# The last four row tiles of an adjacency product, cut in two groups of two instead of three and one

## The reference

```
keep   = u >= 0.1
x_drop = x * keep / 0.9
y      = x + adj @ x_drop
out    = (y - mean(y)) / sqrt(var(y) + 1e-5)      # over the 64 columns of each row
```

## Time and profile before

| | |
|---|---|
| median of 3 runs | 641.93 us (641.93 to 641.95) |
| profiled execution, its own time | 642.16 us |
| its span | 640.2 us |
| TensorE (PE) busy | 510.8 us, 80% |
| TensorE weight loads (PEld) | 263.7 us |
| VectorE busy | 60.8 us, 9% |
| ScalarE busy | 17.0 us, 3% |
| bytes moved by DMA | 274.80 MB, mean 429 GB/s |

### The profile page before, as it was taken

The page is one execution under the profiler, slowest core; times in us unless marked ns, Lnnn a source line. Parts: engine busy times, 40 slices in busy tenths (PEclk is TensorE's granted clock), DMA queues, the critical chain, the costliest instruction groups (busy, mean ns, idle before and its releaser), DMA issues.

```text
span 640.2 us, 7695 instructions
## 1 busy us (share of the span) xinstructions
PE 510.8 (80%) x3458; PEld 263.7 (41%) x3458; DVE 60.8 (9%) x268; ACT 17.0 (3%) x24; POOL 1.1 (0%) x8
## 2 busy tenths in 40 slices
PE   0088798798788787887788878878977977979997
PEld 0044444444443443443444434433433443445435
DVE  1200100100100100010100110010010020020202
ACT  0000000000000000000000000000000000000000
POOL 0000000000000000000000000000000000000000
PEclk9997988988988987989978978978977987979999
DMA  9999999999999999999999999999999999999998
GB/s 385 430 431 447 427 430 450 430 430 447 434 430 424 445 434 404 430 434 439 430 434 447 430 430 450 430 430 440 436 434 399 458 438 407 435 424 431 434 419 354
DMA packets 7348, 274.80 MB, mean 429 GB/s; under 512 B 944, under 2 KB 1072, under 8 KB 1456
## 3 DMA queue, kind: packets, MB, share of 16 engines
q1 hardware_dynamic: 7200, 274.70, 99.5%
q10 hardware_dynamic: 144, 0.03, 0.0%
HBM read 272.63 MB, written 2.10 MB: 429 GB/s over the span
## 4 chain that ended last, share of the span: by engine, by line
DMA 66%; PE 33%; issue 0%; SPq 0%; DVE 0%; ACT 0%; ACTq 0%; DVEq 0%
DMA adj_ring<-adj_blocks 66%; PE acc L234 31%; PE tail_acc L234 2%; PE back L241 0%; SPq L151 0%; PE final L273 0%; SPq L153 0%; DVE x_and_u L342 0%; SPq L172 0%; ACT std L224 0%; DVE acc_sb L280 0%; ACTq L202 0%; DVE stats L336 0%; DVE mean_var L338 0%; DVE rstd L340 0%
## 5 line engine op out<-in xcount | busy, mean ns | idle before, releaser
L234 PE MATMUL acc<-adj_ring,x_and_u 128*64 128x320 f32 x3072 | 463.9, 467 | 99.4 <-ACTq L202 99.4
L234 PEld LDWEIGHTS acc<-adj_ring,x_and_u 128*64 128x64 f32 x3072 | 232.1, 148 | 326.2 <-ACTq L202 107.3
L280 DVE COPY acc_sb<-acc 128x320 f32<-128x320 f32 x24 | 10.7, 486 | 477.0 <-PE acc L234 477.0
L234 PE MATMUL tail_acc<-adj_ring,x_and_u 128*64 128x384 f32 (+1 forms) x256 | 29.1, 382 | 0.9 <-DMA adj_ring<-adj_blocks 0.8
L241 PE MATMUL back<-twofold,acc_sb 128*128 128x64 f32 x126 | 16.8, 280 | 11.9 <-DVE acc_sb L280 11.9
L196 ACT ACT_TABLE_LOAD x10 | 12.8, 1283 | 502.5 <-DMA adj_ring<-adj_blocks 502.5
L241 PEld LDWEIGHTS back<-twofold,acc_sb 128*128 128x128 f32 x126 | 15.0, 191 | 18.8 <-DVE acc_sb L280 18.7
L234 PEld LDWEIGHTS tail_acc<-adj_ring,x_and_u 128*64 128x64 f32 x256 | 15.7, 137 | 13.9 <-issue 9.8
L311 DVE TENSOR_SCALAR x_and_u<-summed,mean,rstd 128x64 f32 (+1 forms) x63 | 15.2, 310 | 0.5
L248 PE MATMUL final<-x_and_u,identity 128*128 128x64 f32 x2 | 0.7, 434 | 13.2 <-DMA x_and_u<-xu 13.2
L289 DVE BATCH_NORM_STATS2 stats<-summed 128x6 f32<-128x64 f32 x63 | 9.3, 213 | 0.4
(11 more groups left out here) (17 smaller groups left out, 7.4 us busy)
## 6 DMA issues: line engine op xcount, KB each, us to landing
adj_ring<-adj_blocks SPq DMA_DIRECT2D x23, 7680.0 KB, 33.3
adj_ring<-adj_blocks SPq DMA_DIRECT2D x11, 5120.0 KB, 36.8
adj_ring<-adj_blocks SPq DMA_DIRECT2D x1, 5760.0 KB, 28.0
adj_ring<-adj_blocks SPq DMA_DIRECT2D x1, 4480.0 KB, 30.0
x_and_u<-xu SPq DMA_DIRECT2D x1, 4096.0 KB, 12.4
adj_ring<-adj_blocks SPq DMA_DIRECT2D x1, 3840.0 KB, 23.3
adj_ring<-adj_blocks SPq DMA_DIRECT2D x1, 3072.0 KB, 30.3
adj_ring<-adj_blocks SPq DMA_DIRECT2D x1, 2560.0 KB, 35.7
```

Source lines behind the costliest of these rows:

```text
L234: return nc.tensor.matmul(into[h * D:(h + 1) * D, 0:cols], x_drop[:, t * D:(t + 1) * D], adj_ring[:, at:at + cols], start=(t < 2), stop=(t ...
L280: last = nc.vector.tensor_copy(acc_sb[:, b * cols:(b + 1) * cols], part[:, 0:cols])
```

## The change

The four row tiles behind the loop are cut into two groups of two. The first comes in four pieces of 24, 18, 14 and 8 k tiles, the second in five of 20, 18, 14, 8 and 4. All products of the tail now stream 256 columns, and a k tile of a piece has 128 KB in both groups. The short chain for the last group now works on two row tiles: the copy is 256 columns wide, `final` holds two row tiles of `x`, and the turning, `bn_stats`, `bn_aggr` and the last `tensor_scalar` run twice; the square root and the reciprocal run once, on two columns. SyncE's second store has two row tiles instead of three, ScalarE's last store two instead of one.

```diff
-TAIL = [(3, [20, 16, 12, 10, 6]), (1, [16, 18, 14, 10, 6])]
+TAIL = [(2, [24, 18, 14, 8]), (2, [20, 18, 14, 8, 4])]
 LAST = len(TAIL) - 1
+LAST_ROWS = TAIL[LAST][0]
...
-            cols = slice(FULL * R * D, (KT - 1) * D)
+            cols = slice(FULL * R * D, (KT - LAST_ROWS) * D)
             sp.dma_start(out_rows[:, cols], normed[:, cols]).then_inc(out_stored, 16)
...
-            nc.scalar.activation(std[:, 0:1], mean_var[:, 1:2], ACT.Sqrt, bias=eps[:]).then_inc(std_ready, 1)
+            nc.scalar.activation(std[:, 0:LAST_ROWS], mean_var[:, :, 1], ACT.Sqrt, bias=eps[:]).then_inc(std_ready, 1)
             act.wait_ge(normed_ready, FULL + LAST + 1)
-            cols = slice((KT - 1) * D, KT * D)
+            cols = slice((KT - LAST_ROWS) * D, KT * D)
...
-            nc.tensor.matmul(final[:, 0:D], identity[:], x_nat[:, (KT - 1) * D:KT * D], start=True, stop=False)
+            nc.tensor.matmul(final[:, 0:LAST_ROWS * D], identity[:], x_nat[:, (KT - LAST_ROWS) * D:KT * D],
+                             start=True, stop=False)
...
-            nc.tensor.matmul(final[:, 0:D], acc_sb[:, 0:P], twofold[:], start=False, stop=True).then_inc(final_ready, 1)
+            for r in range(LAST_ROWS):
+                last = nc.tensor.matmul(final[:, r * D:(r + 1) * D], acc_sb[:, r * P:(r + 1) * P], twofold[:],
+                                        start=False, stop=(r == LAST_ROWS - 1))
+            last.then_inc(final_ready, 1)
...
-            take([tail_acc[LAST]], P, MAIN + FIRST_PIECE[LAST] + len(TAIL[LAST][1]))
+            take([tail_acc[LAST]], LAST_ROWS * P, MAIN + FIRST_PIECE[LAST] + len(TAIL[LAST][1]))
             dve.wait_ge(final_ready, 1)
-            nc.vector.bn_stats(stats[:, 0, :], final[:, 0:D]).then_inc(final_stats, 1)
+            for r in range(LAST_ROWS):
+                last = nc.vector.bn_stats(stats[:, r, :], final[:, r * D:(r + 1) * D])
+            last.then_inc(final_stats, 1)
             dve.wait_ge(final_stats, 1)
-            nc.vector.bn_aggr(mean_var[:], stats[:, 0, :]).then_inc(final_var, 1)
+            for r in range(LAST_ROWS):
+                last = nc.vector.bn_aggr(mean_var[:, r, :], stats[:, r, :])
+            last.then_inc(final_var, 1)
             dve.wait_ge(std_ready, FULL + LAST + 1)
-            nc.vector.reciprocal(rstd[:, 0:1], std[:, 0:1]).then_inc(rstd_ready, 1)
+            nc.vector.reciprocal(rstd[:, 0:LAST_ROWS], std[:, 0:LAST_ROWS]).then_inc(rstd_ready, 1)
             dve.wait_ge(rstd_ready, FULL + LAST + 1)
-            nc.vector.tensor_scalar(normed[:, (KT - 1) * D:KT * D], final[:, 0:D], mean_var[:, 0:1], rstd[:, 0:1],
-                                    ALU.subtract, ALU.mult).then_inc(normed_ready, 1)
+            for r in range(LAST_ROWS):
+                row = KT - LAST_ROWS + r
+                last = nc.vector.tensor_scalar(normed[:, row * D:(row + 1) * D], final[:, r * D:(r + 1) * D],
+                                               mean_var[:, r, 0:1], rstd[:, r:r + 1], ALU.subtract, ALU.mult)
+            last.then_inc(normed_ready, 1)
```

More of the change, by code:

```diff
@@ L106, in build @@
         rstd = sb("rstd", [P, R])
-        mean_var = sb("mean_var", [P, 2])
+        mean_var = sb("mean_var", [P, LAST_ROWS, 2])
         acc = [ps(f"acc{b}", 512) for b in range(SPLIT)]
```

## The result

The changed kernel takes 645.21 us (median of 4 runs: 643.93, 644.67, 645.75, 646.12), the kernel before 641.93 beside it: ratio 1.0049, interval 1.0036 to 1.0061. It is slower, as forecast, but the median lies 0.2 us above the range, and the four runs differ by 2.2 us, where those of before differ by 0.1 (by 0.5 over all its executions in this study, 641.89 to 642.37). In all, 22 executions of the changed kernel were timed in this study, and the median of all of them is 644.81, which is inside the range: of the four here two are among the seven longest, so the 0.2 is partly the draw. The profiled execution is the fastest of the four (643.93, span 642.0); with the forecast of 643.9 its course can be compared step by step.

A forecast was written before the change was run, and what follows sets the result against it. The prediction took the loads of `adj` on queue 1 as the bound, with TensorE behind at the end. Products' end +1.1 and end chain +0.85 gave +1.95 us on 641.93: 643.9, range 643.1 to 645.0.

The forecast's parts named there:

- forecast case: Whole tail: products end 1.1 us later, end chain 0.85 us longer, clock holds; 643.9 us, chance 55%.
- the new idle time ahead of the second group: TensorE, tail: idle about 2.1 us until the second group's first piece lands at 621.2; no loss by itself.
- Bound and path: Loads of `adj` on queue 1 pace the loop; the end runs through third last landing, products, serial chain and store.
- Price of a k tile: TensorE, tail: one product of 256 columns costs 0.216 us, on a straight line between 128 and 384 columns.
- Landings: DMA, tail: pieces land at 2.4 us per 1000 KB; second group at 621.2, 626.7, 631.1, 633.5 and 634.8.
- Products' end +1.1: TensorE, behind the last wait: 26 k tiles of 128 KB end at 636.8, before 635.7; 1.1 us later.
- Chain +0.85: Serial operations and last store after the products: two row tiles instead of one cost 0.85 us more, bounds 0.6 to 1.1.
- The sum, +1.95: Whole kernel: 1.1 us for the products' later end plus 0.85 for the end chain, giving 643.9 from 641.93.
- Rival 1: TensorE, second tail group: clock falls in the new idle time, costing 0.8 us (644.7) or 2.5 (646.4); chance 28%.
- Rival 2: DMA, tail: last pieces land earlier, so the kernel is not slower; 642.5 us if 1.4 us earlier; chance 7%.

The follow-up runs named there:

- The fitted pieces: Changed kernel with the second group cut in eight pieces of 10, 12, 12, 10, 8, 6, 4 and 2 k tiles instead of five: 642.97 us.
- the second of the changed kernel: Second profile of the changed kernel, run again with no edit: the profiled execution took 644.96 us, the run's median was 644.78.
- the one with the longer idle time: Changed kernel with 12 of the 14 k tiles of the first group's third piece not computed: median 644.77 us.

## Why the prediction was wrong

Its forecast case came as worked out, step by step, in 4 of 22 executions; what was wrong is that the case was taken for the likeliest.

**The step that failed** is the new idle time ahead of the second group: "It is no loss by itself". The sum has the pieces and the chain, and nothing for the clock. In 18 of 22 executions there was such a loss: 0.39, 0.61, 1.03 and 1.85 us in the four that were profiled. With 2.2 us of it filled by idle products the median is 643.98, and no execution is above 644.12.

- **Bound and path:** right for the forecast case. Queue 1 stays full (99.2%), the path goes through the landing of the third last piece, the products, the chain and the store. In the four slower profiles the waits behind the second group's first piece are gone, so there the path goes through the landing of that piece, near 621, and all products behind it.
- **Price of a k tile:** 0.216 us forecast; the last 52 matmuls take 5.83, 26 x 0.216 and the last one's run.
- **Landings:** within 0.1 us of the line at all three waits of the fastest profile; the first of them is at 621.03 to 621.39 in the five.
- **Products' end +1.1:** measured +1.0. The forecast worked out 635.7 for the end before, where the rows have 635.86. The fitted pieces take 1.0 of it away by the medians and 0.65 in their profile, so it is mostly or wholly the pieces' size behind the last wait.
- **Chain +0.85:** +0.81 from copy to store. The copy cost +0.13, the matmuls +0.23, `bn_stats` +0.13, the `tensor_scalar` +0.25; `bn_aggr`, which no row showed, +0.07 where +0.10 was taken. The store cost nothing more (1.6 us for 1.7), against my +0.05. The Trainium skill's rule on 512 B (DMA: Bandwidth & Descriptors, Specifications) would have given that.
- **The sum, +1.95:** the two profiled executions differ by 1.77 (643.93 for 642.16). That the forecast of 643.9 is met to 0.03 us in the fastest case is partly luck: the sum is 0.18 too large, and the median from which it was counted, 641.93, lies 0.23 below that profiled execution.
- **The new idle time, "about 2.1 us":** too short for four of the five. It was taken from one execution, in which the tail starts at 605.05. The idle times in the five profiles of the changed kernel are 2.06, 2.97, 3.01, 3.17 and 3.39. The tail's start goes with the clock in the last loop group, as a stretch of it shows, first in the fastest profile of the changed kernel, then in the one with the idle time of 2.06:

```profile
568.00:571.00 3.00, 3.00 (x26) 1.58 (x24) 0.00 (x0) 0.00 (x0) 0.00 (x0) 0.99 0.96 415
```

```profile
568.00:571.00 3.00, 3.00 (x14) 1.36 (x12) 0.00 (x0) 0.00 (x0) 0.00 (x0) 0.50 0.92 399
```

  In both it was 0.50 in the 3 us ahead of that; in one it stayed so for 3 us more, and its tail started 1.5 us later. The step says that the group ahead "doesn't change", and it didn't; but its end was hidden behind the loads before and differs by over a microsecond between executions, and nothing in the time before showed it. The length alone didn't decide: the clock fell at 2.06 us, as long as forecast, and held at 3.39.
- **Rival 1, 28%:** the mechanism was right, and the chance was wrong by far: 18 of the 22 executions are above 644.1, and each of the four profiled ones among them shows the fall, while the one profile at 643.9 doesn't. I had held an idle time of 3.68 without a fall against the two rows of 2.30 and 2.42 with one. The profile before shows that this was its one exception. Its loop has 22 waits of 2.30 to 6.19 us behind the first of 17.43 ahead of any product, and the granted clock was 0.50 in or right behind 21 of them. Four stretches, behind waits of 3.05, 3.37, 2.92 and 3.23 us:

```profile
196.20:199.00 2.80, 2.80 (x12) 1.32 (x14) 0.00 (x0) 0.00 (x0) 0.00 (x0) 0.50 1.08 468
244.60:250.00 5.40, 5.40 (x22) 2.43 (x24) 0.00 (x0) 0.00 (x0) 0.00 (x0) 0.50 1.07 463
438.20:441.20 3.00, 3.00 (x12) 1.44 (x14) 0.00 (x0) 0.00 (x0) 0.00 (x0) 0.50 1.01 437
486.70:492.40 5.70, 5.70 (x22) 2.55 (x24) 0.00 (x0) 0.00 (x0) 0.00 (x0) 0.50 1.07 460
```

  So a fall was the rule, and could be read before the run. Over the loops of all twelve profiles of this study (from 90 us on), none of 8 waits of 2.02 to 2.08 us brought a fall, all 108 of 2.15 to 3.42 did, and 25 of 33 of 3.43 to 3.68. The tail doesn't follow this by length: 2.06 brought one and 3.39 none. Beside my rows stood the Trainium skill (TensorE: Matmul & The Clock Gate, the closing table), which warns only of longer idle times than 2.1 us. By the Trainium skill's warning the clock would have held in the execution with 2.06 us too; it didn't. The idle time of 3.39 us, of the length that it does warn of, kept the clock.
- **Its price:** 0.8 forecast, 0.4 to 1.0 measured, and 2.5 for the longer stretch, 1.85 measured. The size was fair; what wasn't drawn from it is that the median then lies in the middle of the executions, near 645, not at the lowest.
- **Rival 2** (earlier landings): no run shows it; the landing forecast for 621.2 came at 621.03 to 621.39.

Not settled: what decides in which execution the clock falls. 3.39 us of idle time left it up once and 2.06 took it down once, while the loop's waits of 2.02 to 2.08 never did. Nothing was tried that would set when the idle time begins independently of the rest.

## What to carry to other kernels

Where the loads are the bound, TensorE's idle times, and the clock that they cost, stay hidden as long as enough waits for a landing stand behind them. Behind the last wait nothing hides them: count the work that is left when the last pieces land, and cut the pieces so that each one's products last no longer than the next one's transfer (worth 1.0 us with groups of two here, and nothing that could be measured in the kernel before). A wait of 2 to 3 us that a regrouping opens shortly before the end should be taken for a fallen clock, as it was in 18 of 22 executions here, and not for free time; times that spread in separate groups were the sign of it. When rows are picked for and against a rival, count all that the profile has: here 21 of 22 waits spoke for it, and the prediction named two of them beside the only one against. Where an edit lays bare a point of the schedule that used to be hidden, take its position from several profiles.

## What was not expected of the hardware

After idle times of 2.06 to 3.39 us TensorE ran at a granted clock of 0.50 for 3.4 us or less of its work in three profiles and for close to 6 us in one, and in one not at all, with the same program; idle work of 2.2 us in the same place kept it at 1.00 and took the spread from 2.2 to 0.25 us. In two profiles the clock fell more than one us after TensorE had started again (the second of the changed kernel, start at 621.39 and fall near 622.6, and the one with the longer idle time, 621.33 and near 622.4), so the idle time and its price can stand apart in the trace.
